# Attention over edge slots: one fetch of 40 rows for two consecutive nodes in place of 24 rows for one, four consecutive tokens to a partition, and sums over slots by a tree of additions

## The reference, cut to what matters

```python
x = x + conv(_ln_c(x))                 # 16 x 32 x 32 x 128: M = 16384 tokens of 128 channels
t = tokens(x)
t = t + ffn(_ln_t(t))
# in ffn, h = x_flat @ W_gat, 4 heads of 4 values per token (M x 16)
e = leaky_relu(a_src[src] + a_dst[dst], negative_slope=0.2)      # 524288 edges and M self loops
e_max = segment_max(e, dst, num_segments=M)
ee = exp(e - e_max[dst])
denom = segment_sum(ee, dst, num_segments=M)
msg = h[src] * (ee / (denom[dst] + 1e-16))[:, :, None]
agg = segment_sum(msg, dst, num_segments=M)                      # M x 16
scores = layernorm(agg + b_gat).reshape(M, 4, 4).mean(1)         # 4 expert scores per token
topk_s, topk_i = top_k(scores, 2); w = softmax(topk_s)
for ei in range(4):
    g = where(topk_i == ei, w, 0).sum(-1)
    out = out + g[..., None] * (gelu(x @ W1[ei] + b1[ei]) @ W2[ei] + b2[ei])
```

## Time and profile before

| | us |
|---|---|
| median of 3 runs | 2300.07 |
| lowest, highest | 2298.7, 2302.07 |
| span of the profiled execution | 2297.5 |
| its last stage, from POOL's first gather after the extra list step | 1406.9 to 2297.5 |

### The profile page before, as it was taken

One profiled execution on the slowest core, in us unless ns is written; L12 is line 12 of the kernel. 1 busy time (PEld: TensorE's weight loads), 2 busy tenths in 40 slices (PEclk: granted clock), 3 DMA queues, 4 the chain that ended last, 5 costly groups with the idle time before them and its releaser, 6 DMA issues. The chain is left out here.

```text
span 2297.5 us, 16425 instructions
## 1 busy us (share of the span) xinstructions
PE 1086.1 (47%) x4821; PEld 479.8 (21%) x4821; DVE 1594.7 (69%) x3100; ACT 762.8 (33%) x1260; POOL 1212.5 (53%) x1233
## 2 busy tenths in 40 slices
PE   3897878778678887000700102433342425333330
PEld 1233343334533333000300001111111112111110
DVE  6999999995726999999209504364758384747658
ACT  4664846535345554000300002222232324222221
POOL 2000000000066777777777764777777777777771
PEclk8898878787589999555855556766676768676665
DMA  8202031021454322111221611344453535363543
GB/s 297 115 1 74 1 8 38 1 8 39 47 57 110 79 71 71 14 15 29 48 41 29 43 16 41 98 144 121 121 176 85 165 92 176 72 187 73 169 113 100
DMA packets 185735, 182.76 MB, mean 80 GB/s; under 512 B 81580, under 2 KB 164462, under 8 KB 176046
## 3 DMA queue, kind: packets, MB, share of 16 engines
q1 hardware_dynamic: 99262, 88.84, 14.4%
q0 software_dynamic: 43936, 47.85, 12.4%
q10 hardware_dynamic: 42448, 45.04, 6.4%
HBM read 105.23 MB, written 76.40 MB: 79 GB/s over the span
## 5 line engine op out<-in xcount | busy, mean ns | idle before, releaser
L519 POOL DMA_INDIRECT KC<-node_dram,KB x1026 | 1018.4, 993 | 938.8 <-DMA node_dram<-node_out 626.3
L740 PE MATMUL hidden_out<-XT,W 128*128 128x512 f32 x512 | 291.3, 675 | 540.8 <-ACT ARENA_A L956 539.9
L745 PE MATMUL hidden_out<-ARENA_A,W 128*128 128x512 f32 x512 | 264.7, 642 | 24.9 <-ACT ARENA_A L956 24.9
L956 ACT ACTIVATE ARENA_A<-hidden_out,b1c 128x512 f32<-128x512 f32 x256 | 174.2, 687 | 294.5 <-PE hidden_out L740 293.9
L740 PEld LDWEIGHTS hidden_out<-XT,W 128*128 128x128 f32 x512 | 97.3, 211 | 689.5 <-ACT ARENA_A L956 570.1
L1523 DVE TENSOR_TENSOR KB<-XG,MB 128x3072 bf16<-128x3072 f32 x20 | 67.1, 3354 | 163.5 <-DMA XG<-rest_dram,win_i 100.7
L1649 DVE TENSOR_SCALAR KB<-MB 128x16 f32<-128x16 f32 (+1 forms) x33 | 5.7, 172 | 238.3 <-DMA KC<-payload,slot_idx 126.8
L1800 DVE SCALAR_TENSOR_TENSOR XG<-XT,KB,XG 128x128 f32<-128x128 f32 x512 | 144.3, 347 | 14.9 <-DMA XT<-ye_dram 11.2
L959 ACT ACTIVATE ARENA_A<-hidden_out,b2c 128x512 f32<-128x512 f32 x128 | 87.9, 687 | 185.5 <-PE hidden_out L745 185.5
L1026 ACT ACTIVATE TA<-KB 128x400 f32<-128x400 f32 x32 | 16.2, 507 | 373.3 <-DVE KB L1656 373.2
L745 PEld LDWEIGHTS hidden_out<-ARENA_A,W 128*128 128x128 f32 x512 | 98.3, 207 | 182.4 <-ACT ARENA_A L956 103.1
(11 more groups left out here) (401 smaller groups left out, 2232.0 us busy)
## 6 DMA issues: line engine op xcount, KB each, us to landing
ye_dram<-ARENA_D ACTq DMA_DIRECT2D x32, 1024.0 KB, 4.0
XT<-ye_dram SPq DMA_DIRECT2D x32, 1024.0 KB, 13.5
KC<-node_dram,KB POOLq DMA_INDIRECT x1026
payload<-XT SPq DMA_DIRECT2D x1, 11520.0 KB
payload<-KC SPq DMA_DIRECT2D x115, 90.0 KB, 1.8
XG<-x_dram SPq DMA_DIRECT2D x32, 256.0 KB, 11.3
out_dram<-XG ACTq DMA_DIRECT2D x32, 256.0 KB, 3.4
KA<-in_L_ffn_edge_index_dram SPq DMA_DIRECT2D x1, 2048.0 KB, 9.0
```

What stands on the lines that cost most here:

```text
L519: pool.indirect_dma_start(row_buf[h][:, t, :], None, node_dram, bass.IndirectOffsetOnAxis(ap=KB[:, col:col + 1].bitcast(I32), axis=0)).the ...
L740: last = pe.matmul(PF[i % 2][:, :], W1[:, m // 2, (m % 2) * P:(m % 2) * P + P], XT[:, n * CHUNK:(n + 1) * CHUNK], start=True, stop=True)
L745: last = pe.matmul(PF[i % 2][:, :], W2[:, 2 * m + kk, :], HH[:, 2 * m + kk, :], start=kk == 0, stop=kk == 1)
L956: act.activation(HH[:, m, :], PF[i % 2][:, :], ACT.Gelu, bias=b1c[:, m:m + 1]).then_inc(S["hid_out"], 1)
```

## The change

The slot fetch takes 40 rows for two consecutive nodes, so a group has two fetches (`WINS`) in place of four. For this the two nodes must be neighbours in the list: partition p now holds tokens 512n + 4p + j. All loads and stores by token follow (`x1_chunks`, `out_chunks`, `node_dram`, `adst_dram`), PE's transposes of the experts' outputs take every fourth column, and the tables of starts and degrees are turned by 48 small matmuls in place of three transposes. Both fetch buffers now lie in `KC`; the products go to `KA`.

Since both nodes of a pair look at the same 40 rows, each term exists twice: 640 terms in place of 400, of which a mask that is now two instructions rules out those of the other node. The earlier maximum and the earlier sums are no longer a 25th slot but are kept apart and folded in by small instructions. The sum over 40 slots is made by three additions of halves (1280, 640, 320 elements) and a reduction of the last five; the sum of the exponentials stays a reduction. The exponential is two instructions (320 and 336 elements).

```diff
-SLOTS = 24
+SLOTS = 40
 NODES = 4
+SHARED = 2
+WINS = NODES // SHARED
+SETS = P // SHARED
...
-        x1_chunks = x1_dram.rearrange("(s t p) c -> s p t c", t=TPC, p=P)
-        out_chunks = out.rearrange("b h w c -> (b h w) c").rearrange("(s t p) c -> s p t c", t=TPC, p=P)
+        x1_chunks = x1_dram.rearrange("(s p t) c -> s p t c", t=TPC, p=P)
+        out_chunks = out.rearrange("b h w c -> (b h w) c").rearrange("(s p t) c -> s p t c", t=TPC, p=P)
...
-                for t in range(NODES):
-                    at = n * NODES + t
+                for t in range(WINS):
+                    at = n * WINS + t
                     pool.indirect_dma_start(
-                        slot_rows[h][:, t, 0:SLOTS, :].rearrange("p k w -> p (k w)"), None, listed,
+                        slot_rows[h][:, t, :, :].rearrange("p k f -> p (k f)"), None, listed,
                         bass.IndirectOffsetOnAxis(ap=slot_idx[:, at:at + 1], axis=0)).then_inc(slots_gathered[h], 16)
...
             def attention(n):
                 act.wait_ge(S["e_ready"], n + 1)
-                act.activation(exp_out, e_buf, ACT.Exp).then_inc(S["e_exp"], 1)
+                for into, args in exp_parts:
+                    last = act.activation(into, args, ACT.Exp)
+                last.then_inc(S["e_exp"], 1)
...
-                then(red(run_max[:, cols, :], terms.rearrange("p c k g -> p c g k"), AX.X, ALU.max))
-                return tt(terms, terms, bc(run_max[:, cols, :], 2, [P, NODES, TERMS, HEADS]), ALU.subtract)
+                then(red(top_now, every(terms).rearrange("p c k g -> p c g k"), AX.X, ALU.max))
+                then(tt(best_of, best_of, best, ALU.max))
+                then(tt(by_node(kept_args), best, best_of, ALU.subtract))
+                then(tt(best, best_of, best_of, ALU.max))
+                return tt(every(terms), every(terms), bc(top_now, 2, [P, NODES, SLOTS, HEADS]), ALU.subtract)
...
-                then(tt(split(rows[:, :, :, HEADS:]), split(rows[:, :, :, HEADS:]),
-                        bc(exps.rearrange("p c k g -> p (c k) g"), 3, [P, NODES * TERMS, HEADS, EXPERTS]), ALU.mult))
-                then(tt(so_far, so_far, denom[:, cols, :], ALU.mult))
-                settle()
-                red(denom[:, cols, :], exps.rearrange("p c k g -> p c g k"), AX.X, ALU.add)
-                return red(agg[:, cols, :], rows[:, :, :, HEADS:].rearrange("p c k f -> p c f k"), AX.X, ALU.add)
+                for i in range(SHARED):
+                    last = tt(prod[:, i, :, :].rearrange("p m (g x) -> p m g x", g=HEADS), parts,
+                              bc(exps[i], 3, [P, ROWS, HEADS, EXPERTS]), ALU.mult)
+                held = agg[:, cols, :].rearrange("p c (g x) -> p c g x", g=HEADS)
+                then(last)
+                then(tt(held, held, bc(kept, 3, [P, NODES, HEADS, EXPERTS]), ALU.mult))
+                then(tt(denom[:, cols, :], denom[:, cols, :], kept, ALU.mult))
+                each = prod.rearrange("p i (w k) f -> p (i w) (k f)", k=SLOTS)
+                n = SLOTS
+                while n % 2 == 0:
+                    n //= 2
+                    then(tt(each[:, :, 0:n * HE], each[:, :, 0:n * HE], each[:, :, n * HE:2 * n * HE], ALU.add))
+                then(red(sum_now, each[:, :, 0:n * HE].rearrange("p c (k f) -> p c f k", f=HE), AX.X, ALU.add))
+                for i in range(SHARED):
+                    last = red(by_set(den_now)[:, i, :, :], exps[i].rearrange("p (w k) g -> p w g k", k=SLOTS),
+                               AX.X, ALU.add)
+                then(last)
+                then(tt(by_node(denom[:, cols, :]), by_node(denom[:, cols, :]), by_set(den_now), ALU.add))
+                return tt(by_node(agg[:, cols, :]), by_node(agg[:, cols, :]), by_set(sum_now), ALU.add)
```

More of the change, by code:

```diff
@@ new lines, in _, with mark_unused @@
+            by_node = lambda ap: ap.rearrange("p (w i) x -> p i w x", i=SHARED)
+            by_set = lambda ap: ap.rearrange("p (i w) x -> p i w x", i=SHARED)
+            every = lambda ap: ap.rearrange("p i (w k) g -> p (i w) k g", k=SLOTS)
+            def mark_unused(ends, then):
+                then(tt(past_end[:, 1:, :].rearrange("p i (w k) -> p i w k", k=SLOTS),
+                        bc(bc(slot_iota[:, :], 1, [P, WINS, SLOTS]), 1, [P, SHARED, WINS, SLOTS]),
+                        bc(ends.rearrange("p (w i) -> p i w", i=SHARED), 3, [P, SHARED, WINS, SLOTS]), ALU.is_ge))
+                return tt(unused, past_end[:, 1:, :], past_end[:, 0:SHARED, :], ALU.is_equal)
@@ new lines, in sums @@
+            def sums(rows, cols, then):
+                parts = rows[:, :, :, HEADS:].rearrange("p w k (g x) -> p (w k) g x", g=HEADS)
+                for i in range(SHARED):
[11 more added lines that the diff above has]
+                then(red(sum_now, each[:, :, 0:n * HE].rearrange("p c (k f) -> p c f k", f=HE), AX.X, ALU.add))
+                for i in range(SHARED):
+                    last = red(by_set(den_now)[:, i, :, :], exps[i].rearrange("p (w k) g -> p w g k", k=SLOTS),
+                               AX.X, ALU.add)
+                then(last)
+                then(tt(by_node(denom[:, cols, :]), by_node(denom[:, cols, :]), by_set(den_now), ALU.add))
+                return tt(by_node(agg[:, cols, :]), by_node(agg[:, cols, :]), by_set(sum_now), ALU.add)
@@ L1710, in _ @@
                 assert done[0] == REST_OPS, done
[L1712 removed]
+            EXTRA_OPS = 22
+            link(dve.memset(past_end[:, 0, :], 1.0))
             with dve.Fori(0, extra_list_steps(dve)) as i:
```

142 lines of the change are left out of this document (82 added, 60 removed).

## The result

The changed kernel takes 2288.7 us (median of 4 runs, 2286.31 to 2289.08); the kernel before, on the same chip, 2299.5 (2298.7 to 2302.07). The ratio is 0.9948, with a 95% interval of 0.9933 to 0.9962: the change gains 10.8 us, half a per cent. The forecast was 2285, with 2274 to 2296 as its own range.

A forecast was written before the change was run, and what follows sets the result against it. POOL was taken to bound the kernel before, the loop of DVE and ACT after it. Gains of 4.5, 12.8 and 7.9 us, less 2 x 5.4 lost at the end, gave 2285 us, range 2274 to 2296.

The forecast's parts named there:

- The bound moved: Last stage: pace passes from POOL (94.3 us per four-group super stage) to the loop of DVE and ACT (103.3).
- the four intervals: Times between successive groups' exponentials in one super stage of four groups, together 103.3 us.
- DVE's group: DVE's time per group in the last stage, added up by instruction: 15.3 us in place of 9.9, 5.4 more.
- to group 4's exponential: Start of the last stage, POOL pacing the first super stage: group 4's exponential at 1557.7, 4.5 us gained.
- six super stages: Groups 4 to 28, paced by the DVE and ACT loop: 103.3 us each in place of 105.4, 12.8 gained.
- group 28's exponential to group 30: Near the end: the waits for loads of `ye_dram` go, less DVE's growth, 7.9 us gained.
- the lock: Long DVE instructions with two SBUF inputs stretch POOL's gathers: 2.2 us per group, just POOL's spare, so nothing moves.
- POOL's 77.5 us: POOL's saving up to group 30's fetch, 31 x 2.5 us, the whole gain if POOL kept the pace.
- The first (POOL keeps the pace): Rival: in the last stage DVE and ACT are over 9 us per super stage quicker than costed; 2233; chance 7%.
- The second (DVE held by POOL): Rival: POOL holds DVE at five long instructions per group, 1.8 us per group, 29 us: 2314; chance 12%.
- The third (ACT's interval grows): Rival: ACT's `hidden` takes one us more per chunk, 14 us: 2299, no change; chance 14%.
- The fourth (a cheaper group): Rival: DVE's small instructions overlap better and a group costs 1 us less: 2269; chance 9%.

The follow-up runs named there:

- e8: Changed kernel with ACT's `hidden` cut in two, six of its twelve steps behind each even exponential and six behind each odd one: 2268.5 us.
- e6: Kernel before with ACT's `hidden` cut in two, six of its twelve steps behind each even exponential and six behind each odd one: 2300.2 us.
- e9: Changed kernel with one memset of 720 elements per group in POOL's queue ahead of the slot fetches: 2291.2 us.
- e2: Changed kernel with one more DVE reduction of 864 contiguous elements in each group's sums: 2305.8 us.
- e1: Changed kernel without leaky relu, second product, first addition of the tree and most of the last subtraction, so it computes something else: 2234.6 us.
- e4: Changed kernel with one strided reduction over all 40 slots in place of the three additions and small reduction: 2298.2 us.
- e10: Changed kernel with `hidden` split six and six steps and one strided reduction in place of the additions: 2259.2 us.
- e12: Changed kernel with `hidden` split into eight and four steps and one strided reduction in place of the additions: 2255.9 us.
- e11: Changed kernel with ACT's `hidden` split into eight steps behind even exponentials and four behind odd ones: 2264.7 us.
- e7: Kernel before with the new token order alone, keeping four fetches of 24 rows and the old sums: 2296.8 us.

## Why the prediction was right, point by point

**The bound moved.** Right. POOL's 80 issues per 100 us fell; the four intervals were costed at 22.9, 15.3, 20.6 and 44.5 and are 22.4, 15.4, 20.1 and 44.5. e8 (17 to 20 us from ACT's order, against 0 in e6) and e9 (2.5 to 4 us, not 23, from POOL's) confirm it. e2 does so by its total (16 to 18 exposed groups against 16), though the trace puts part of it elsewhere than the prediction did.

**DVE's group.** 15.3 costed, 15.41 measured. Elementwise prices from two rows were right to a hundredth (1493, 825 and 492 ns for the tree, 1.49, 0.82 and 0.49 costed). One term was mis-sized: the two reductions from PSUM read 320 elements each, not 160, and take 0.89 us together in place of 0.64. The long reductions came out shorter (1287 ns for 1.33).

**The stretches of the sum**, as differences from before, in us:

| stretch | costed | measured |
|---|---|---|
| to group 4's exponential | -4.5 | +3.0 |
| six super stages | -12.8 | -15.5 |
| group 28's exponential to group 30 | -7.9 | -8.4 |
| groups 30, 31 and the end | +10.8 | +10.5 |
| mask counted twice | -0.8 | |
| sum | -15.2 | -10.4 |

The forecast missed by 3.7 us, and that it came so near is in part luck. The first stretch was costed 7.5 us too short and had the wrong sign; the other terms together, the correction for the mask included, were too long and took 2.7 us of this back. 1.0 more came back from the 2.6 us that were added to the span: each single run is only 1.6 to 2.1 us longer than its own span, in the changed kernel's profiled run 1.6, and the rest of the 2.6 was the distance of that one execution from the median.

**The six super stages, one by one.** The prediction compared means, 104.3 for POOL against 103.3 for the loop. Before, heavy and light super stages took 111 and 99 to 100 us. The change gained 6.5, 9.0 and 8.4 us in the heavy ones and lost 3.3, 3.2 and 2.0 in the light ones. In these the loop is now slower than POOL had been with all its fetches. The mean of a super stage came out right, 102.9 against 103.3, but each single one moved by two to nine us.

**The step that failed: the lock and the first super stage.** The prediction saw the lock in the earlier trace rows, sized it at up to 2.2 us per group, and then wrote that nothing in the sum moves, because POOL has that much spare. That holds where the loop paces. In the first super stage, by its own words, POOL paces, and there every stretch of POOL counts. Group 3's exponential came at 1520.5 in place of 1513.2. Of these 7.3 us, 2.0 are the later arrival at the extra list step (costed at 0.2: 1.4 of it arose ahead of it, behind a load that DVE waits for, and 0.6 in the steps from there to L1786, the memset among them). The 1.4 is no cost that the change is shown to have: DVE gets that load at 1381.9 in this profile, at 1379.4 to 1381.3 in those of the changed kernel's eight variants, and at 1380.2 to 1380.9 in the kernel before and its three. Four groups of 18 gathers then took 4.7 us more than at 1.25 us per DMA, 1.2 per group, and 0.6 lie between group 3's last fetch and its exponential. e1, which takes away the longest of the additions and two passes over 640 elements, and e4, which takes away all three additions, win back much of it: three groups take 75.0 us in e1 and 76.2 in e4, against 78.3. The upper end had been sized high (measured are 27 us over the stage, 0.9 per group); what failed was the place where it counts.

**Where POOL's 77.5 us went.** Group 30's first fetch was issued at 2228.15 before and at 2194.24 after, 33.9 us earlier. 2.0 went at the start, about 27 to the lock (591 DMAs at 1003 ns where 957 were paid), 15 to the waits for DVE behind the light groups. Of the 34 that are left DVE's start of group 30 shows 21 (2252.01 to 2231.05), and its last two groups give back 10.5.

**The end.** The load of `ye_dram` isn't waited for any more, as costed from where its stores are issued.

**The rivals.** The first (POOL keeps the pace) is out, by e9. The second (DVE held by POOL) too: L1716 took 1493 ns beside a POOL that was issuing, the price of the earlier trace rows, and L1706, with one input in PSUM, has 1484 in the changed kernel, in e4 and in e8 alike. In group 31 the three additions run when POOL's last DMA has long ended (2229.4), and take the 2.88 us that they took beside it at 1732.21:

```profile
2268.09 2.88 DVE L1716 TENSOR_TENSOR KA<-KA 128x1280 f32<-128x1280 f32 x3
```

The Trainium skill (Trainium Architecture — The Big Picture, What this means for kernel authors) calls the contention of the two an exclusive lock; by these rows it is one that only POOL is seen to wait for: 956 to 999 ns there, nothing on DVE. The third (ACT's interval grows) is out, 22.4 us against 22.6 before. The fourth (a cheaper group) is out, at 15.41.

## What to carry to other kernels

Cost each term against the engine that paces its own stretch, not against the one that paces the stage: a slowdown of the queue with slack "costs nothing" only behind the point where the pace has passed. When two loops lie within some per cent of each other, an edit is worth nothing, its full size or its negative depending on which is ahead (the split: 0 and some 20 us; the tree: some 10 us for and some 10 against), so after a change of bound the edits that had been no gain before are worth a new run. And an engine that may be only two buffers ahead can't save what a light group gives it: compare the counts of neighbouring stretches, not only their mean.

## What the runs showed of the hardware that was not expected

- An indirect DMA costs POOL the same 0.95 us and 0.30 behind it whether a partition gets 20, 480 or 800 values (the earlier trace rows and the rows of 1403.86 and 1430.59 above). The landing differs: from issue to landing 2.5 us in the median for 20 values, 3.7 to 4.0 for 480 before, 4.7 for 800.
- The lock's mean effect on a gather is small: 956 ns in the kernel before, 961 to 963 where the longest passes with two SBUF inputs have 640 elements (e1, e4, e10, e12), 990 to 999 with the tree (the changed kernel, e2, e8, e9, e11). A single DMA beside the tree took 2.22 us.
- Weight loads of 128 columns taken at every fourth position took 212 ns in place of 155 (e7).
- A reduction over a stride has no single price per element: 1600 elements 3161 ns and 640 elements 1287 (2.0 ns per element), but 2560 elements 4430 (1.73). The straight line through two smaller sizes overshot by 0.6 us. A reduction over neighbouring elements costs no more than an elementwise pass (864 elements 1053 ns in e2, by the line through 400 and 1600 elements 1055), while L1696, at a stride of 16 bytes, took 1287 ns for 640 where the line gives 821:

```profile
L1711 DVE TENSOR_REDUCE pad_out<-KC 128x1 f32<-128x864 f32 x32 | 33.7, 1053 | 1.1
```

The Trainium skill (SBUF — State Buffer, Door 1: The DMA port swizzle) says that SBUF has lines of 16 bytes and that each access that crosses to a new line pays. A stride of 16 bytes does so at every element, and the two rows agree. The same place gives 4 fp32 values as how far one can stride for free; at a stride of exactly 4 the rows show that it isn't free. From PSUM the reductions over the same stride (L1719, 320 elements) took 486 ns, the elementwise price.
